# Linear attention: half heads in blocks of their own, features through device memory

## Chip, core and metric

The kernel is one program on one core of a Trainium2 chip. The metric is the device time of one execution in microseconds. PE is TensorE, DVE VectorE, ACT ScalarE, POOL GpSimd, SP SyncE, which here only issues DMAs. The granted clock is the share of TensorE's full clock.

## What is computed

Four chunks of 512 tokens go through a block of a Macaron shape. The lines below leave out reshapes and the other layers.

```python
x = L0_attn_hidden_states                       # 4 x 512 tokens x 512
x = x + 0.5 * _L0_ffn_ref(_layernorm(x), ...)   # spline lookup
x = x + _L0_attn_ref(_layernorm(x), ...)        # linear attention: what the change touches
x = x + 0.5 * _L0_ffn_ref(_layernorm(x), ...)
x = x + 0.5 * _L1_ffn_ref(_layernorm(x), ...)   # Hadamard feed-forward
x = x + _L1_attn_ref(_layernorm(x), ...)        # differential softmax attention
x = x + 0.5 * _L1_ffn_ref(_layernorm(x), ...)

def _L0_attn_ref(hidden_states, Wq, bq, Wk, bk, Wv, bv, Wo, bo, rand_matrix):
    # 16 query heads, 8 key and value heads, 32 dimensions each
    q = (hidden_states @ Wq.T + bq) ...; k = ... ; v = ...
    q = q * cos + _rotate_half(q) * sin         # halves of 16: concat(-x2, x1)
    k = k * cos + _rotate_half(k) * sin
    n = jnp.sqrt(jnp.sum(x * x, axis=-1, keepdims=True))
    x = x / jnp.maximum(n, 1e-06)
    p = jnp.einsum('...d,ed->...e', x, R)       # R: rand_matrix, 16 x 32
    feats = jnp.concatenate([jnp.sin(p), jnp.cos(p)], axis=-1) / math.sqrt(F)
    kv = jnp.einsum('bhsf,bhsd->bsfd', kp, v)   # per token, over the heads
    out = jnp.einsum('bhsf,bsfd->bhsd', qp, kv)
    return out @ Wo.T + bo
```

## The kernel before

The program keeps all 2048 tokens in SBUF and runs in three stretches. Setup (0 to 230 us) turns and mixes the weights and routes the first spline layer. The body of the linear attention runs as `b_tensor`, `b_vector`, `b_scalar`, `b_pool`, `b_sync`, called with i = -1 to 3 (b_sync with 0 to 3). The rest, from about 750 us, is the second layer (`solo_*`, `c_*`), 67% of the span.

Every engine's instruction order is written out by hand and semaphores join them. A run i has up to four roles (`b_roles`): the chunk `now` = i is scored and written out, `new` = i + 1 is projected and turned into features, `look` = i + 2 goes through the first spline layer, and `back` = i - 1 is routed for the next one.

A run has two parts. The y-loop goes over y = 0 to 16 (16 pairs of groups of 16 tokens). For `now`, at each y TensorE makes scores (L1299), VectorE masks them (L1623, same token only), and at y + 1 TensorE weights the values (L1312) into one PSUM bank, `SUM_BANK`; every four y ScalarE and VectorE read it as high and low halves (`sums`, L1455 and L1631), for which `weighted` waits. For `new`, TensorE computes six projections of 128 rows, first the keys' two blocks, then the queries' four (`project`, 12 f16 matmuls in L1184). ScalarE adds the bias (L1461), TensorE swaps the half heads with a constant matrix (`rotate`, L1330), GpSimd multiplies by the cosines (L1549), VectorE by the sines and adds (`rope`, L1638 and L1639), GpSimd squares (L1552), and TensorE sums the squares per head (`length`, L1336). Then `lengths`, `inverse` (Ln, Exp on ScalarE) and `refine` (L1643 to L1651) give the inverse lengths. VectorE's list holds, besides, the spline lookup for `look` (place at y = 6, slope at 8, value at 11) and the token sums and routing for `back` (picks at y = 1 and 2, ends at y = 3 where i >= 2).

In the tail, for each block z, TensorE spreads the inverse lengths over the rows (L1345) and projects the block on the random matrix (L1348). ScalarE copies the spread (L1475). VectorE multiplies the two and reduces the angle (`angle`, L1659, L1663, L1664), ScalarE takes the sine and the high half (L1477, L1480), VectorE the low half (`low`, L1671). Sine and cosine rows are made of one block at once, with a phase that differs by row: 16 rows of sine and 16 of cosine of each head. Between them stand the values (`value`, L1690), output rows (`output`, `residual`, L1679), the norm and the transposes of the next chunk's input (`look`; L2068, L1851) and routing for `back`. The next run's first score comes behind these on TensorE.

The features are laid from the blocks into the stacks `ks` and `qs` (three parts of 32 rows: high, high or low, low or high; heads along the free axis) by direct DMAs from SBUF to SBUF (`b_spread`, L1570): per chunk 18 on SP's queue and 18 on GpSimd's, 64 KB each. ScalarE regroups `ks` into `ksg` (`keys`, L1488). The values go out to device memory (L1605) and come back in another order (L1609) on SP's queue, between the spreads of the first and of the second half of the queries.

## Time and profile before

| | us |
|---|---|
| median of 3 runs (2273.76 to 2275.56) | 2275.51 |
| the profiled execution | 2269.64 |
| its span, first to last instruction | 2267.8 |
| TensorE busy | 1996.4 (88%) |
| VectorE busy | 1269.0 (56%) |
| ScalarE busy | 727.9 (32%) |
| GpSimd busy | 258.9 (11%) |
| granted clock, mean | 0.926 |

In timeline rows the columns are start, duration, engine, line, operation, operands, count, and in brackets the idle time before it and what ended it. An f32 matmul shows as two records. Run i = -1 has its first projection at 230 us and its first spread at 275; the first scores of i = 0, 1, 2, 3 start at 319.6, 419.5, 530.3 and 631.5 us.

### The profile page before, as it was taken

The page shows a single profiled execution, that of the slowest core. Times are in us where ns is not written, and L with a number is a line of the kernel's source. Part 1 is how long each engine was busy: PE and PEld are TensorE (multiplying, and loading weights), DVE is VectorE, ACT ScalarE, POOL GpSimd, SP SyncE. Part 2 cuts the span into 40 slices and gives each one's busy share as a digit, 9 for nine tenths or more (in the row PEclk, how much of TensorE's full clock was granted, in tenths as well). Part 3 has the DMA queues.
Part 4 walks back from the last instruction along what each step waited for, and adds up shares of the span by engine and source line. Part 5 has one row for each costly group of instructions (what it writes and reads, how often), then busy time and mean ns, then how long its engine had stood idle before and what let it go on. Part 6 is the DMA issues. An engine that isn't in the chain of part 4 may idle for free.

```text
span 2267.8 us, 29080 instructions
## 1 busy us (share of the span) xinstructions
PE 1996.4 (88%) x11854; PEld 940.2 (41%) x11854; DVE 1269.0 (56%) x2323; ACT 727.9 (32%) x1131; POOL 258.9 (11%) x236
## 2 busy tenths in 40 slices
PE   4774868887863899999999999999999999999999
PEld 3442333334332444444444444444444444444444
DVE  5777457676576455554565356636564456623322
ACT  4552242432421222232244223522343234411211
POOL 3630221322210000001000100001000100000000
PEclk7886778978966999999999999999999999999999
DMA  7224030212222222212111111111111111133321
GB/s 262 93 75 174 1 61 15 47 35 26 44 65 103 72 96 93 96 53 75 47 57 47 56 47 44 60 65 38 38 66 38 65 47 57 57 102 102 112 96 71
DMA packets 87680, 158.71 MB, mean 70 GB/s; under 512 B 44342, under 2 KB 51324, under 8 KB 82812
## 3 DMA queue, kind: packets, MB, share of 16 engines
q1 hardware_dynamic: 85244, 152.14, 21.0%
q0 software_dynamic: 2304, 4.72, 1.0%
q8 instruction: 94, 1.54, 0.3%
q14 instruction: 38, 0.31, 0.0%
HBM read 128.52 MB, written 18.87 MB: 65 GB/s over the span
## 4 chain that ended last, share of the span: by engine, by line
PE 49%; DVE 4%; ACT 2%; issue 1%; ACTq 0%; DVEq 0%
PE ps L1184 26%; PE ps L1936 12%; PE ps L2450 2%; PE ps L2469 1%; DVE arena L2614 1%; PE ps L2446 1%; PE ps L2452 1%; PE ps L2396 1%; PE ps L2487 1%; PE ps L2471 1%; PE ps L2473 1%; PE ps L2478 1%; PE ps L2476 1%; PE ps L2393 1%; DVE arena L1991 0%
## 5 line engine op out<-in xcount | busy, mean ns | idle before, releaser
L1184 PE MATMUL ps<-arena 128*128 128x512 f16 (+1 forms) x4512 | 1013.7, 379 | 22.8 <-DVE arena L1991 12.9
L1184 PEld LDWEIGHTS ps<-arena 128*128 128x128 f16 x4512 | 434.8, 98 | 541.2 <-issue 45.3
L1936 PE MATMUL ps<-arena 128*128 128x512 f16 x1536 | 343.8, 379 | 12.5 <-DVE arena L2019 9.3
L1936 PEld LDWEIGHTS ps<-arena 128*128 128x128 f16 x1536 | 146.6, 97 | 185.9 <-DVE arena L2019 12.1
L1991 DVE SCALAR_TENSOR_TENSOR arena<-arena,ps 128x512 f32<-128x512 f32 x128 | 87.9, 687 | 208.7 <-ACT arena L1958 208.1
L1958 ACT ACTIVATE arena<-ps,arena 128x512 f32<-128x512 f32 x128 | 87.8, 686 | 358.5 <-PE ps L1184 358.4
L2543 ACT ACTIVATE arena<-ps 128x1024 f32<-128x1024 f32 (+3 forms) x128 | 90.3, 706 | 254.1 <-PE ps L2452 254.1
L2648 DVE CAST arena<-arena 128x1024 f16<-128x1024 f32 (+3 forms) x128 | 66.2, 517 | 150.4 <-ACT arena L2543 148.3
L2614 DVE TENSOR_REDUCE arena<-ps 128x2 f32<-128x256 f32 (+3 forms) x128 | 99.6, 820 | 65.0 <-PE ps L2396 65.0
L2019 DVE SCALAR_TENSOR_TENSOR arena<-ps,arena 128x512 f32<-128x512 f32 x64 | 44.0, 688 | 134.5 <-PE ps L1936 134.3
L2000 DVE SCALAR_TENSOR_TENSOR arena<-ps,arena 128x512 f32<-128x512 f32 x128 | 95.8, 748 | 39.1 <-PE ps L1184 39.0
L2650 DVE TENSOR_TENSOR arena<-arena 128x1024 f16<-128x1024 f32 (+3 forms) x128 | 111.4, 871 | 4.4
L2594 POOL TENSOR_TENSOR arena<-arena 128x512 f16<-128x512 f32 x32 | 37.1, 1160 | 624.9 <-ACT arena L2521 624.9
L1982 DVE TENSOR_TENSOR arena<-arena 128x512 f16<-128x512 f32 x128 | 90.9, 711 | 4.0 <-ACT arena L1950 4.0
L1950 ACT ACTIVATE arena<-arena 128x512 f16<-128x512 f32 x128 | 79.8, 624 | 17.5 <-DVE arena L2000 17.5
L2598 POOL TENSOR_TENSOR arena<-arena 128x512 f32<-128x512 f32 x16 | 19.0, 1187 | 581.5 <-DVE arena L2661 581.5
L1851 PE MATMUL ps<-arena 128*128 128x128 f32 x192 | 33.2, 333 | 55.1 <-ACT arena L2068 55.1
L1623 DVE TENSOR_TENSOR arena<-ps,arena 128x256 f32<-128x256 f32 x128 | 47.9, 417 | 56.4 <-PE ps L1299 55.7
L2450 PE MATMUL ps<-arena 32*128 32x512 f16 (+3 forms) x768 | 72.9, 293 | 0.0
L2518 ACT ACTIVATE arena<-ps 128x512 f32<-128x512 f32 x32 | 19.1, 598 | 166.6 <-PE ps L1184 166.6
L731 PE MATMUL ps<-arena 128*128 128x128 f32 x240 | 44.1, 325 | 31.6 <-DVE arena L968 18.9
L1312 PE MATMUL ps<-arena 128*32 128x64 f32 x1024 | 41.9, 294 | 28.3 <-DVE arena L1623 14.3
(268 smaller groups left out, 2435.4 us busy)
## 6 DMA issues: line engine op xcount, KB each, us to landing
arena<-wug_dram SPq DMA_DIRECT2D x128, 512.0 KB, 3.3
arena<-wd_hi_dram SPq DMA_DIRECT2D x16, 1024.0 KB, 5.0
arena<-wd_lo_dram SPq DMA_DIRECT2D x16, 1024.0 KB, 7.3
wug_dram<-arena SPq DMA_DIRECT2D x4, 2048.0 KB, 15.7
arena<-arena SPq DMA_DIRECT2D x72, 64.0 KB, 2.9
arena<-arena POOLq DMA_DIRECT2D x72, 64.0 KB, 2.7
arena<-_attn_hidden_states_dram SPq DMA_DIRECT2D x4, 1024.0 KB, 12.3
arena<-in_L_ffn_W_up_dram SPq DMA_DIRECT2D x8, 512.0 KB, 5.0
```

The source lines that it names most:

```text
L1184: ins = pe.matmul(out, left[a](c), right[b](c), start=(at == 0), stop=(at == 3 * n - 1))
L1936: ins = pe.matmul(k.ps[:, bank, :], act[x][:, slot, cols], wd[y][:, f, :], start=(f == 0 and m == 0), stop=(f == 7 and m == 2))
L1950: e.activation(k.act_hi[:, g % ACT_SLOTS, :], k.prod[:, g % 2, :], ACT.Copy).then_inc(s["f_hi"], 1)
L1958: e.activation(k.th[:, g % 2, :], k.ps[:, GATE_BANK, :], ACT.Tanh, scale=k.wscale[:, FB + a:FB + a + 1])\
L1982: e.tensor_tensor(k.act_lo[:, g % ACT_SLOTS, :], k.prod[:, g % 2, :], k.act_hi[:, g % ACT_SLOTS, :], ALU.subtract)\
L1991: e.scalar_tensor_tensor(out=th, in0=th, scalar=1.0, in1=k.ps[:, GATE_BANK, :], op0=ALU.add, op1=ALU.mult)\
L2000: e.scalar_tensor_tensor(out=k.prod[:, g % 2, :], in0=k.ps[:, UP_HALF_BANK, :], scalar=k.wscale[:, a:a + 1], in1=th, op0=ALU.mult, op1=ALU ...
L2450: pe.matmul(k.ps[:, bank, queries], x[rows, 4 + b, keys], y[rows, b, queries], start=False, stop=False)
L2543: e.activation(k.p32[:, t % 2, :, queries], k.ps[:, 0:2, queries], ACT.Exp, scale=SCORE).then_inc(s["c_exp"], 1)
L2614: e.tensor_reduce(k.mx[:, u, 4 * b + 2 * j:4 * b + 2 * j + 2], k.ps[:, bank:bank + 2, 0:(u + 1) * P], AXX, ALU.max).then_inc(s["c_max"], 1)
L2648: e.tensor_copy(k.p_hi[:, t % 2, :, queries], k.p32[:, t % 2, :, queries]).then_inc(s["c_p_hi"], 1)
L2650: e.tensor_tensor(k.p_lo[:, t % 2, :, queries], k.p32[:, t % 2, :, queries], k.p_hi[:, t % 2, :, queries], ALU.subtract).then_inc(s["c_p_l ...
```

## The change

Each projection block now holds one half (16 dimensions) of eight heads: `halves_of` reorders the rows of the query and key weights and of their biases at load. A pair of blocks (a = 0 keys, 1 and 2 queries) holds the two halves of the same heads on the same partitions. So the rotation needs no matmul: VectorE reads the projection in PSUM twice, adding the bias and multiplying by cosine and sine (with the scale folded into the tables), and GpSimd adds or subtracts across the pair. The projection on the random matrix is two matmuls that accumulate, for eight heads; the groups a = 0 and 1 are issued at y = 14 and 15. One product with the lengths serves sine block and cosine block, which are blocks of their own with a phase each. The lengths are spread for three pairs instead of six blocks.

Features go to the stacks through a tensor `feat` in device memory: a store per block and part, a load per stack part, the load waiting for its stores. SP carries the high parts, GpSimd the low parts. On SP the values are stored behind the third and fourth block's stores and loaded behind the sixth's, before the last queries' loads. ScalarE's keys(2) and keys(3) stand behind the last feature. The sums use two banks in turn.

```diff
-    parts = [("ident", ident), ("had", had), ("rot", rot), ("cos", np.cos(ang)),
+    parts = [("ident", ident), ("had", had), ("cos", np.cos(ang) * unit),
...
-    load_nat(0, [(rows_of(d["L0_attn_Wq"])[:, 0:2], 2), (rows_of(d["L0_attn_Wq"])[:, 2:4], 2)])
-    load_nat(1, [(rows_of(d["L0_attn_Wk"]), 2), (rows_of(d["L0_attn_Wv"]), 2)])
+    load_nat(0, [(halves_of(d["L0_attn_Wq"], z), 1) for z in range(4)])
+    load_nat(1, [(halves_of(d["L0_attn_Wk"], z), 1) for z in range(2)] + [(rows_of(d["L0_attn_Wv"]), 2)])
...
-    for j in range(8):
-        sp.dma_start(k.rt[32 * (j // 2):32 * (j // 2) + 32, 16 * j:16 * j + 16],
-                     d["L0_attn_rand_matrix"].rearrange("e d -> d e")).then_inc(s["b_in"], 16)
+    for h in range(8):
+        for half in range(2):
+            sp.dma_start(k.rt[16 * h:16 * h + 16, half, 16 * h:16 * h + 16],
+                         d["L0_attn_rand_matrix"].rearrange("e d -> d e")[16 * half:16 * half + 16])\
+                .then_inc(s["b_in"], 16)
...
+    V.link(e.tensor_scalar(k.bqk, k.bqk, W_SCALE * A_SCALE, None, ALU.mult))
...
-SUM_BANK = 5
+SUM_BANK = (4, 5)
-ROT_BANK = 4
-LAST_BANK, LAST_KEY = (2, 3), 4
+LAST_BANK, LAST_KEY = (2, 3), 7
-ROT_AT = (2, 3, 5, 6, 8, 9)
+TURN_AT = (14, 15)
...
-        if y % 4 == 0 and y:
-            pe.wait_ge(s["b_ot_lo"], TPC * now + y // 4)
+        if y % 4 == 0 and y >= 8:
+            pe.wait_ge(s["b_ot_lo"], TPC * now + y // 4 - 1)
...
         if t >= 2:
-            pe.wait_ge(s["b_qf"], 6 * new + t - 1)
+            pe.wait_ge(s["b_rope"], 6 * new + t - 1)
...
-    def rotate(z):
-        pe.wait_ge(s["b_qf"], 6 * new + z + 1)
-        need(pe, s["b_rope"], 6 * new + z)
-        pe.matmul(k.ps[:, ROT_BANK, :], k.c["rot"], k.qf[:, z, :], start=True, stop=True).then_inc(s["b_rot"], 1)
...
-    def turns(z):
-        if new is None:
-            return
-        if z == 0:
+    def turned(a):
+        pe.wait_ge(s["b_rot"], 6 * new + 2 * a + 2)
+        if a == 0:
+            pe.wait_ge(s["b_rope"], 6 * (new + 1))
+        else:
+            need(pe, s["b_y"], 3 * new + a - 1)
+        for half in range(2):
+            ins = pe.matmul(k.ps[:, PROJ_BANK[a % 2], :], k.rt[:, half, :], k.qr[:, 2 * a + half, :], start=(half == 0),
+                            stop=(half == 1))
+        ins.then_inc(s["b_proj"], 1)
+
+    def spread(a):
+        if a == 0:
             pe.wait_ge(s["b_r"], new + 1)
-        need(pe, s["b_spread"], 6 * new + z)
-        pe.matmul(k.ps[:, WIDE_BANK, :], k.spread[:, z * P:(z + 1) * P], k.r2, start=True, stop=True).then_inc(s["b_p"], 1)
-        if z >= 2:
-            pe.wait_ge(s["b_y"], 6 * new + z - 1)
-        pe.matmul(k.ps[:, PROJ_BANK[z % 2], :], k.rt, k.qr[:, z, :], start=True, stop=True).then_inc(s["b_proj"], 1)
+            if now is not None:
+                pe.wait_ge(s["b_ot_lo"], TPC * now + 3)
+        need(pe, s["b_spread"], 3 * new + a)
+        pe.matmul(k.ps[:, WIDE_BANK, :], k.spread[:, a * P:(a + 1) * P], k.r2, start=True, stop=True).then_inc(s["b_p"], 1)
...
-    for z in range(4):
-        turns(z)
-        value(z)
-    turns(4)
+    if new is not None:
+        spread(0)
+    value(0)
+    value(1)
+    if new is not None:
+        spread(1)
+    value(2)
+    value(3)
+    if new is not None:
+        spread(2)
+        turned(2)
     output(0)
-    turns(5)
     output(1)
...
 # b_scalar, tail
-    for z in range(4):
-        turns(z)
+    spread(0)
+    feature(0)
+    spread(1)
+    feature(1)
+    feature(2)
+    spread(2)
+    feature(3)
+    feature(4)
     keys(0)
     keys(1)
-    turns(4)
+    feature(5)
     keys(2)
     keys(3)
-    turns(5)
...
 # b_pool
+        for a in range(3):
+            e.wait_ge(s["b_rope"], 6 * new + 2 * a + 2)
+            for half, op in enumerate((ALU.subtract, ALU.add)):
+                z = 2 * a + half
+                e.tensor_tensor(k.qr[:, z, :], k.qr[:, z, :], k.qf[:, 2 * a + 1 - half, :], op).then_inc(s["b_rot"], 1)
+            for z in (2 * a, 2 * a + 1):
+                e.wait_ge(s["b_rot"], 6 * new + z + 1)
+                need(e, s["b_nsum"], 6 * new + z - 1)
+                e.tensor_tensor(k.q2[:, z % 2, :], k.qr[:, z, :], k.qr[:, z, :], ALU.mult).then_inc(s["b_sq"], 1)
+        b_low_spread(k, e, new)
...
+def b_store(k, eng, part, z, sem):
+    f = (k.f_hi, k.f_lo)[part]
+    eng.dma_start(k.d["feat"][part, z // 2][:, z % 2], f[:, z, :]).then_inc(sem, 16)
+
+def b_load(k, eng, part, a, rows, sem):
+    stack, heads = (k.ks, slice(0, 8)) if a == 0 else (k.qs, slice(8 * a - 8, 8 * a))
+    eng.dma_start(stack[32 * rows:32 * rows + 32, heads, :], k.d["feat"][part, a].rearrange("h s e t -> (s e) h t"))\
+        .then_inc(sem, 16)
+
+def b_low_spread(k, e, i):
+    need(e, s["b_qs2"], 32 * i)
+    for a in range(3):
+        for z in (2 * a, 2 * a + 1):
+            e.wait_ge(s["b_f_lo"], 6 * i + z + 1)
+            b_store(k, e, 1, z, s["b_lo_out"])
...
+        e.wait_ge(s["b_lo_out"], 96 * i + 32 * (a + 1))
+        b_load(k, e, 1, a, 1 if a else 2, s["b_qs2" if a else "b_ks2"])
...
 # b_sync
+    for a in range(3):
+        for z in (2 * a, 2 * a + 1):
+            sp.wait_ge(s["b_f_hi"], 6 * i + z + 1)
+            b_store(k, sp, 0, z, s["b_hi_out"])
...
+        if a == 1:
+            need(sp, s["b_s"], PAIRS * i)
+            sp.wait_ge(s["b_v_in"], TPC * (i + 1))
+            need(sp, s["b_vr"], 128 * i)
+            sp.dma_start(scratch.rearrange("(u p) n -> p u n", p=P), k.v0).then_inc(s["b_v_out"], 16)
+        if a == 2:
+            need(sp, s["b_pv"], PAIRS * i)
+            sp.wait_ge(s["b_v_out"], 16 * (i + 1))
+            for h in range(8):
+                sp.dma_start(k.vr[GROUP * h:GROUP * h + GROUP], scratch[:, 32 * h:32 * h + 32]
+                             .rearrange("(g t) d -> t g d", t=GROUP)).then_inc(s["b_vr"], 16)
+        sp.wait_ge(s["b_hi_out"], 96 * i + 32 * (a + 1))
+        for rows in ((0, 2) if a else (0, 1)):
+            b_load(k, sp, 0, a, rows, s["b_qs" if a else "b_ks"])
...
 # b_vector
     def rope(z):
-        e.wait_ge(s["b_rot"], 6 * new + z + 1)
-        e.wait_ge(s["b_cos"], 6 * new + z + 1)
-        V.link(e.tensor_tensor(k.qf[:, z, :], k.ps[:, ROT_BANK, :], k.c["sin"], ALU.mult))
-        e.tensor_tensor(k.qr[:, z, :], k.qr[:, z, :], k.qf[:, z, :], ALU.add).then_inc(s["b_rope"], 1)
+        e.wait_ge(s["b_qk_done"], 6 * new + z + 1)
+        if z == 0:
+            need(e, s["b_proj"], 3 * new)
+        bias = k.bqk[:, ORDER[z]:ORDER[z] + 1]
+        for to, table in ((k.qr, "cos"), (k.qf, "sin")):
+            ins = e.scalar_tensor_tensor(out=to[:, z, :], in0=k.ps[:, PROJ_BANK[z % 2], :], scalar=bias, in1=k.c[table],
+                                         op0=ALU.add, op1=ALU.mult)
+        ins.then_inc(s["b_rope"], 1)
...
     def angle(z):
...
+        a, half = z // 2, z % 2
+        ang, turns = k.ang[:, half, :], k.turns[:, a % 2, :]
+        if half == 0:
+            e.wait_ge(s["b_proj"], 3 * new + a + 1)
+            e.wait_ge(s["b_spread"], 3 * new + a + 1)
+            e.scalar_tensor_tensor(out=turns, in0=k.ps[:, PROJ_BANK[a % 2], :], scalar=float(1 / (2 * np.pi)), in1=turns,
+                                   op0=ALU.mult, op1=ALU.mult).then_inc(s["b_y"], 1)
+            e.wait_ge(s["b_y"], 3 * new + a + 1)
         need(e, s["b_f_lo"], 6 * new + z - 1)
-        V.link(e.tensor_scalar(ang, turns, k.c["phase"], ROUND, ALU.add, ALU.add))
+        V.link(e.tensor_scalar(ang, turns, PHASE[half], ROUND, ALU.add, ALU.add))
...
-            if y - 1 in ROT_AT:
-                rope(ROT_AT.index(y - 1))
+            if y - 1 in QK_AT:
+                rope(QK_AT.index(y - 1))
...
+        d["feat"] = nc.dram_tensor("feat_dram", (2, 3, 8, 2, 16, CH), F16).ap()
```

## Rows read from the trace of the kernel before

**Rows 1.** Windows: stretch, length, busy us of each engine (instructions), clock, DMA share, GB/s.
```profile
core 0: us, PE busy (x) PEld busy (x) DVE busy (x) ACT busy (x) POOL busy (x), PEclk, DMA share, GB/s
319.60:376.00 56.40, 47.76 (x409) 21.45 (x412) 33.17 (x75) 8.28 (x13) 13.04 (x12) 0.91 0.00 1
530.30:588.00 57.70, 47.39 (x369) 18.65 (x368) 38.23 (x84) 10.62 (x19) 12.58 (x12) 0.87 0.00 1
631.50:672.00 40.50, 24.46 (x333) 14.77 (x336) 31.40 (x80) 9.04 (x16) 0.00 (x0) 0.58 0.01 1
750.00:2267.00 1517.00, 1469.19 (x8698) 665.82 (x8696) 780.12 (x1299) 464.91 (x722) 75.76 (x64) 1.00 0.20 67
```

**Rows 2.** Timeline of SP's queue in the setup.
```profile
7.41 0.92 SPq L627 DMA_DIRECT2D arena<-in_L_attn_Wq_dram  x2
163.55 7.09 SPq L667 DMA_DIRECT2D arena<-_L_attn_rand_matrix_dram  x8
198.00 0.52 SPq L651 DMA_DIRECT2D wd_hi_dram<-arena  x1
```

**Rows 3.** Timeline of the y-loop of i = 0, PE and POOL.
```profile
328.20 1.13 PE L1330 MATMUL ps<-arena 128*128 128x512 f32 x2
330.05 2.77 PE L1184 MATMUL ps<-arena 128*128 128x512 f16 x12
331.75 1.04 POOL L1552 TENSOR_TENSOR arena<-arena 128x512 f32<-128x512 f32 x1 [5.88 <-DVE arena L1639]
332.74 1.09 POOL L1549 TENSOR_TENSOR arena<-arena 128x512 f32<-128x512 f32 x1
...
357.82 0.67 PE L1312 MATMUL ps<-arena 128*32 128x64 f32 x16 [2.08 <-DVE arena L1631]
359.90 2.05 PE L1330 MATMUL ps<-arena 128*128 128x512 f32 x2 [1.41 <-DVE arena L1639]
370.96 0.64 PE L1312 MATMUL ps<-arena 128*32 128x64 f32 x16 [2.34 <-DVE arena L1631]
376.25 1.12 PE L1345 MATMUL ps<-arena 24*128 24x512 f32 x2
```

**Rows 4.** Timeline: first spreads, a rotation, an angle, a first score of other runs.
```profile
274.95 2.07 PE L1345 MATMUL ps<-arena 24*128 24x512 f32 x2 [4.65 <-DVE arena L1651]
550.39 2.05 PE L1330 MATMUL ps<-arena 128*128 128x512 f32 x2 [5.96 <-DVE arena L1639]
590.09 2.07 PE L1345 MATMUL ps<-arena 24*128 24x512 f32 x2
594.21 0.69 DVE L1659 SCALAR_TENSOR_TENSOR arena<-ps,arena 128x512 f32<-128x512 f32 x1 [2.65 <-PE ps L1348]
631.48 1.03 PE L1299 MATMUL ps<-arena 96*128 96x256 f16 x4
```

**Rows 5.** Timeline of the tail of i = 0: VectorE, ScalarE and the next first score.
```profile
378.79 0.69 DVE L1659 SCALAR_TENSOR_TENSOR arena<-ps,arena 128x512 f32<-128x512 f32 x1 [1.09 <-PE ps L1348]
...
404.06 1.99 ACT L1488 ACTIVATE arena<-arena 96x1024 f16<-96x1024 f16 x2
406.63 0.69 DVE L1659 SCALAR_TENSOR_TENSOR arena<-ps,arena 128x512 f32<-128x512 f32 x1 [1.76 <-ACT arena L1475]
409.36 0.63 ACT L1480 ACTIVATE arena<-arena 128x512 f16<-128x512 f32 x1
410.03 0.69 DVE L1671 SCALAR_TENSOR_TENSOR arena<-arena 128x512 f16<-128x512 f32 x1 [0.85 <-ACT arena L1480]
419.50 0.38 PE L1299 MATMUL ps<-arena 96*128 96x256 f16 x2 [0.21 <-issue]
```

**Rows 6.** DMA issues: tensors, queue, count, KB each, median us from issue to landing.
```profile
arena<-arena SPq DMA_DIRECT2D x72, 64.0 KB, 2.9
arena<-arena POOLq DMA_DIRECT2D x72, 64.0 KB, 2.7
values_dram<-arena SPq DMA_DIRECT2D x4, 512.0 KB, 3.1
arena<-values_dram SPq DMA_DIRECT2D x32, 64.0 KB, 4.1
```

**Rows 7.** Timeline of SP's queue, the loads of the values in i = 0.
```profile
407.85 4.01 SPq L1609 DMA_DIRECT2D arena<-values_dram  x8
```

More of the change, by code:

```diff
@@ L41 @@
 BIG = 1.0e30
+PHASE = (0.0, 0.25)
 def host_constants():
@@ L1647, in refine @@
         e.wait_ge(s["b_n"], new + 1)
-        need(e, s["b_p"], 6 * new)
+        need(e, s["b_p"], 3 * new)
         V.link(e.tensor_tensor(t, n2, r0, ALU.mult))
```

170 lines of the change are left out of this document (66 added, 104 removed).

## Prediction

> **What bounds the kernel now.** I read the stage windows first. From 750 us to the end TensorE is busy 1469.2 of 1517 us at a full clock, and no line of that part changes [rows 1]. What the change touches lies between 230 and 672 us: the five runs of the linear-attention body, i = -1 to 3. Each is a y-loop (scores, masks, sums of one chunk beside projections of the next) and a tail (features, spreads, output rows, next transposes). In the y-loop of i = 0 TensorE is busy 47.8 of 56.4 us, VectorE 33.2; in that of i = 3, which has no new chunk, VectorE 31.4 of 40.5 [rows 1]. So with a new chunk the order on TensorE sets the loop, with VectorE not far behind. In the tails TensorE has room and VectorE's in-order stream does not: from the first angle to its last low half it runs 378.79 to 410.72, and what interrupts it is ScalarE [rows 5]. The chain of waits on the page reaches back only to about 985 us, so for this stretch I use the timeline.
>
> **Change part by part.**
>
> *Rotation.* Six `rotate` matmuls (L1330) per new chunk go. A pair of f32 records takes 1.13 us at full clock and 2.05 at half [rows 3], so i = 0 loses about 5 x 1.1 + 2.05 = 7.6 us of TensorE time and the 1.41 us wait in front of the last one. The six ScalarE evacuations (L1461) go as well. VectorE keeps twelve passes a chunk: two fused reads of PSUM per block replace two passes. The new form is that of L1659, 0.69 us [rows 5], like the pass it replaces. GpSimd keeps twelve passes at 1.04 to 1.09 us [rows 3], but four now follow each pair of blocks, 4.3 us behind the second block.
>
> *Sum banks.* Bank 5 alternates with bank 4, so `weighted` at y = 4, 8, 12 no longer waits for the sums before it. Those waits are 2.08 and 2.34 us in i = 0 [rows 3].
>
> *Projection onto the random features.* Six f32 matmuls stay, as two-matmul groups, and two of the three groups move into the loop at y = 14 and 15: four matmuls, 4 x 1.12 (form of L1345 [rows 3]) = 4.5 us on TensorE. They wait only for GpSimd's rotated halves, and lie beside the length, Ln/Exp and refine work of VectorE and ScalarE. Three of the six spread matmuls go from the tail.
>
> *y-loop of i = 0, queued by hand in the new order.* Gross 7.6 + 1.4 + 4.4 - 4.5 = 8.9 us. VectorE takes part of it back, because its lookahead work (place, slope, value) is untouched and now meets masks and rope: by my queueing the last rope pair ends at 351.6, `length(5)` at 359.9, the refinement at 366.4, `turned(1)` at 369.3, and the first spread starts at 370.0 where it was 376.25 [rows 3]. Gain 6.2 (bounds 3 and 9). i = 1 has the same order plus token sums: 6.0. i = -1 has no masks, its first spread stood at 274.95 behind the refinement [rows 4]; rope without a matmul between brings it to 267.7: 7.2. i = 2 had the longest stall: rotate(1) waited 5.96 us for VectorE, which stood in route picks and ends [rows 4]. Now rope runs in front of those ends, so projections and lengths go on: first spread at about 578.5 against 590.09, gain 11.6 (bounds 5 and 14; this is the least certain term). i = 3: no new chunk, only the bank change. VectorE is its bound, and the mask of the same y comes just ahead of the sums: 2.0 (bounds 0.5 and 4).
>
> *Tails.* The first angle needs one spread and one copy instead of spread, copy and projection: 378.79 - 376.25 = 2.5 becomes 1.8, gain 0.7 (1.3 in i = -1). Each odd block saves the product with the lengths, 0.69 plus a step: 3 x 0.7 = 2.1 us of VectorE per chunk. The 1.76 us in which angle(5) waited for ScalarE's copy goes too [rows 5]. Against this, keys(2) and keys(3), 1.99 us for two, now stand behind the last Sin and copy and in front of the table load and root that start the next transposes. From first angle to first score it was 419.50 - 378.79 = 40.7; requeued 39.3, so 1.4 each for i = -1, 0, 1. i = 2 has no scatter or norm work on VectorE, and runs at the angle-Sin-copy-low rhythm; there all of the cut shows: the start, 594.21 - 590.09 = 4.1, becomes 2.6, and 4.3 comes off the rest up to 631.48 [rows 4], gain 5.8 (bounds 2 and 8).
>
> *Features through device memory.* Instead of 36 direct spreads of 64 KB per chunk there are 12 stores of 128 KB and 9 loads of 256 KB, on the same two queues: SP issues 6 + 6 instead of 18, GpSimd 6 + 3 instead of 18. A load now waits for its store. Nearest rows: a store to the values takes 3.1 us, a load from them 4.1, a direct spread 2.9 (SP) and 2.7 (GpSimd) [rows 6]. So low half to landed stack: 0.6 + 3.1 + 0.5 + 4.1 = 8.3 us. For the keys the cover is 10 us and more: keys(0) stands behind block 4's copy. For the last queries it is thin. Name T the end of the last feature copy, 409.99 before [rows 5]. On SP the eight value loads, 4.01 us of issue [rows 7], now stand behind the last store and ahead of the query loads, which are so issued at T+5 to T+6, behind their 128-byte pieces, and land at T+10 to T+13. TensorE asks for the queries at T + 9.5 + 2.0 = T+11.5. Cost 0 to 3 us in each of i = -1, 0, 2 (in 1 the route work covers it); I take 0.5 each, 1.5, because the same 768 KB landed before that first score when issued to within 4 us of it. If the cover were gone each us of landing is a us of time.
> The trace shows 3.1 and 4.1 us for the two legs; the Trainium skill (DMA: Bandwidth & Descriptors, Anatomy of one DMA) puts about 2 us of fixed cost on each DMA, most of it the receipt from the target, longest for device memory. That speaks against this change: two such legs where one was. With 2.0 us each the way would be about 6 us, under the cover all the same.
>
> *Setup.* Three more weight loads at 0.46 us (0.92 for two), one more vector and a 0.2 us scaling: 0 to 1.9 us, I take 0.8, as the loads behind are a backlog of transfers. The eight random-matrix loads become sixteen: 7.09 us become at most 14, from 163.55, with the next issue not before 198.00 [rows 2]: hidden.
>
> **Sum.** i = -1: 7.2 + 1.3 + 1.4 = 9.9. i = 0: 6.2 + 0.7 + 1.4 = 8.3. i = 1: 6.0 + 0.7 + 1.4 = 8.1. i = 2: 11.6 + 5.8 = 17.4. i = 3: 2.0. Together 45.7, less 1.5 and 0.8: 43.4 us. The profiled execution took 2269.6 us (span 2267.8), so it would be 2226. The median of the runs shown is 2275.5, 5.9 above it; the forecast is for such a median: 2275.5 - 43.4 = 2232.
>
> **Rivals.**
> 1. *VectorE becomes the bound of the loops.* For: 38.2 of 57.7 us busy in i = 2 [rows 1], and its programme order is a fixed list in which one blocked step holds masks and rope. Against: its passes don't grow. It would hold the loops to a third of the gain (31.0 to 10), tails as forecast: 43.4 - 21 = 22, 2253.
> 2. *The last queries come late.* Landing at T+14 to T+15 costs about 3 more in three tails: 2241.
> 3. *TensorE's clock gives it back.* It was granted 0.91 in i = 0's loop and 0.58 in i = 3's, where it idled [rows 1]; a rotate at the lower of its two levels (1.2 GHz against 2.4) took 2.05 for 1.13, and a projection would take twice its 2.77 [rows 3]. If four of the six projections in each of three loops fell there: 12 x 2.8 = 34, 2266. For: a loop with fewer matmuls leaves more gaps. Against: the gaps that go are TensorE's own waits.
> 4. *Slower than before: loads move at the pace of the old pieces.* Were a 256 KB load four times a direct spread, 4 x 2.9 = 11.6 us [rows 6], and two of them served one after the other, the queries would land at T + 6 + 23 = T+29, 17.7 past the need, in four tails: 71 - 43 = 28 slower, 2303. It decides when the landing is later than T+22 (11 us a chunk). Against: bytes are not what those 2.9 us are made of, since the store of the values moves 512 KB in 3.1 us [rows 6].
> 5. *The gross gain shows in full*, as loops are less tied to VectorE than I queue them: 8.9 for 6.2 in i = 0 and so on, about 15 more: 2217.
> 6. *It does not do what it says*: scores wait anyhow for something unchanged (the transposes of the next chunk). Then only loops gain and tails nothing: 31 + 2 - 2.3, close to 2243; it lies inside the forecast.
>
> **How the numbers follow.** Forecast with 6 and its near surroundings 0.55, rival 1 0.2, rival 2 0.08, rival 3 0.05, rival 4 0.04, rival 5 0.08. Two in ten may be left out: I cut rivals 3 and 4 and the outer halves of 1 and 5. Range 2212 to 2256, which also holds the unknown costs: loops 3 to 9 and 5 to 14, landing 0 to 3 three times, setup 0 to 1.9. About 0.2%, 4.6 us, is what a measurement of this kernel can tell from no change. Faster 0.93 (all but rival 4 and a part of 3), same 0.03, slower 0.04.
>
> **What would show it.** Right: no matmul of the rotation's form; first score of i = 0 about 9 us earlier and that of i = 3 about 41 earlier; first score idle behind transposes or route work, not behind a DMA; first spread right behind the refinement or the second projection group; sums' waits gone at y = 4, 8, 12. Wrong: TensorE idle before a first score until a load of features lands; ScalarE's keys waiting on loads; VectorE without idle time through a y-loop; a granted clock below 0.85 in the loops of i = 0 to 2. The largest error would be in i = 2's loop.

## The result and the profile after

The changed kernel takes 2237.16 us (median of 4 runs, 2231.76 to 2240.6) against 2274.81 for the kernel before (4 runs): ratio 0.9834, 95% interval 0.9821 to 0.9846, a gain of 37.7 us (35 to 41). The forecast was 2232 and a gain of 43.4. The profiled execution of after took 2238.54 us (span 2236.7), that of before 2269.64, so the two profiles differ by 31.1 only; where the other 6.6 probably lie is told with the clock below.

The windows of the body and of the part that the change doesn't touch, after (columns as in [rows 1]):
```profile
core 0: us, PE busy (x) PEld busy (x) DVE busy (x) ACT busy (x) POOL busy (x), PEclk, DMA share, GB/s
237.10:274.70 37.60, 33.66 (x120) 14.10 (x120) 19.66 (x38) 1.85 (x3) 13.85 (x12) 0.86 0.00 0
315.50:367.20 51.70, 47.48 (x409) 21.86 (x409) 33.09 (x74) 3.53 (x7) 13.88 (x12) 0.90 0.01 1
509.00:561.00 52.00, 44.76 (x381) 18.24 (x380) 39.35 (x87) 6.70 (x13) 13.50 (x12) 0.89 0.01 1
596.60:637.80 41.20, 25.04 (x337) 15.25 (x338) 31.80 (x81) 9.74 (x17) 0.00 (x0) 0.58 0.02 3
720.00:2236.00 1516.00, 1468.20 (x8679) 664.96 (x8677) 778.37 (x1297) 463.52 (x721) 75.76 (x64) 0.99 0.20 67
```
The y-loop of i = 0 is 51.6 us long where it was 56.6, that of i = 2 52.1 where it was 59.8. VectorE is busy for about as long as in [rows 1] (33.1 for 33.2 us, 39.4 for 38.2), TensorE in i = 0 too (47.5 for 47.8), in a shorter loop. TensorE's waits for the low half of the sums are gone, but in i = 2 a weighted sum now waits for its mask:
```profile
526.28 0.65 PE L1322 MATMUL ps<-arena 128*32 128x64 f32 x16 [3.71 <-DVE arena L1651]
```

The timeline of after, the points that answer to [rows 4] and [rows 5] (start, duration, engine and line; L1195 is the projections' line, L1361 the spread, L1309 the score, L1498 the feature copy):
```profile
237.10 1.01 PE L1195 MATMUL ps<-arena 128*128 128x512 f16 x2 [1.50 <-DVE arena L1900]
274.75 1.12 PE L1361 MATMUL ps<-arena 24*128 24x512 f32 x2 [0.43 <-DVE arena L1683]
315.55 0.58 PE L1309 MATMUL ps<-arena 96*128 96x256 f16 x2 [0.68 <-issue]
367.16 1.12 PE L1361 MATMUL ps<-arena 24*128 24x512 f32 x2
409.60 0.38 PE L1309 MATMUL ps<-arena 96*128 96x256 f16 x2 [2.32 <-DMA arena<-feat_dram]
...
596.58 0.80 PE L1309 MATMUL ps<-arena 96*128 96x256 f16 x3 [2.47 <-DMA arena<-feat_dram]
```
From such points of both traces comes this table. T is the end of the last feature copy, as in the prediction; "feed" is TensorE's first projection behind the loop of i = 3. Gains in us, predicted and measured:

| part | before | after | predicted | measured |
|---|---|---|---|---|
| setup, to the first projection | 230.4 | 237.1 | -0.8 | -6.7 |
| loop to the first spread, i = -1 | 44.6 | 37.65 | 7.2 | 6.9 |
| the same, i = 0 | 56.6 | 51.6 | 6.2 | 5.0 |
| the same, i = 1 | 58.5 | 51.6 | 6.0 | 6.9 |
| the same, i = 2 | 59.8 | 52.1 | 11.6 | 7.7 |
| first score to feed, i = 3 | 42.5 | 41.2 | 2.0 | 1.3 |
| first spread to first angle, four times | 14.9 | 7.4 | 4.2 | 7.5 |
| first angle to T, four times | 121.2 | 101.6 | | 19.6 |
| T to the first score, four times | 45.6 | 57.5 | | -11.9 |
| the two above together (landing included) | 166.8 | 159.1 | 7.0 | 7.7 |
| sum to the feed | 674.0 | 637.8 | 43.4 | 36.2 |
| feed to the end | 1593.9 | 1599.0 | 0 | -5.1 |

From the first projection to the feed, the stretch that the change works in, 443.6 us became 400.7: 42.9 gained for 44.2 forecast. The parts are further off than their sum.

The DMA issues of after, which answer to [rows 6]:
```profile
arena<-feat_dram SPq DMA_DIRECT2D x24, 256.0 KB, 4.7
...
feat_dram<-arena POOLq DMA_DIRECT2D x24, 128.0 KB, 3.7
arena<-feat_dram POOLq DMA_DIRECT2D x12, 256.0 KB, 4.1
...
values_dram<-arena SPq DMA_DIRECT2D x4, 512.0 KB, 4.0
arena<-values_dram SPq DMA_DIRECT2D x32, 64.0 KB, 4.1
```
A store and a load of the features take 3.7 and 4.1 to 4.7 us, near the 3.1 and 4.1 taken from the values: larger DMAs are not slower in proportion to their size, and rival 4 is out.

### The profile page after: what moved, and what is told of

It is laid out like the page before. It is cut to its first block, busy times and chain, and to the rows that moved or that the text cites. A ratio compares the mean times of both kernels' runs of the same rounds, so it can differ in the third digit from the quotient of the medians.

```text
span 2236.7 us, 28766 instructions
## 1 busy us (share of the span) xinstructions
PE 1958.3 (88%) x11782; PEld 931.0 (42%) x11782; DVE 1260.7 (56%) x2312; ACT 705.0 (32%) x1095; POOL 246.1 (11%) x200
## 4 chain that ended last, share of the span: by engine, by line
PE 49%; DVE 4%; ACT 2%; issue 1%; ACTq 0%; DVEq 0%
PE ps L1195 27%; PE ps L1970 12%; PE ps L2484 2%; PE ps L2503 1%; DVE arena L2648 1%; PE ps L2480 1%; PE ps L2486 1%; PE ps L2430 1%; PE ps L2521 1%; PE ps L2505 1%; PE ps L2507 1%; PE ps L2512 1%; PE ps L2510 1%; PE ps L2427 1%; DVE arena L2025 0%
## 5 line engine op out<-in xcount | busy, mean ns | idle before, releaser
L1195 PE MATMUL ps<-arena 128*128 128x512 f16 (+1 forms) x4512 | 1017.5, 381 | 41.0 <-DVE arena L1724 18.8
L1195 PEld LDWEIGHTS ps<-arena 128*128 128x128 f16 x4512 | 434.0, 99 | 557.0 <-issue 38.5
L1970 PEld LDWEIGHTS ps<-arena 128*128 128x128 f16 x1536 | 146.6, 97 | 185.8 <-DVE arena L2053 12.1
L741 PE MATMUL ps<-arena 128*128 128x128 f32 x240 | 46.7, 340 | 35.3 <-DVE arena L979 16.4
L1651 DVE TENSOR_TENSOR arena<-ps,arena 128x256 f32<-128x256 f32 x128 | 47.2, 416 | 42.3 <-PE ps L1309 41.5
L1322 PE MATMUL ps<-arena 128*32 128x64 f32 x1024 | 41.9, 293 | 25.8 <-DVE arena L1651 25.6
```

Source lines behind the costliest of these rows:

```text
L1195: ins = pe.matmul(out, left[a](c), right[b](c), start=(at == 0), stop=(at == 3 * n - 1))
L1970: ins = pe.matmul(k.ps[:, bank, :], act[x][:, slot, cols], wd[y][:, f, :], start=(f == 0 and m == 0), stop=(f == 7 and m == 2))
```

## The experiments

Times are medians, ratios are to the kernel before as run beside each. All of them start from the changed kernel unless it is said. What each kernel's one profiled execution shows is set beside the median here, cut at the first projection and at the feed, since the stretch behind the feed takes one of two lengths some 5 us apart, whatever the edit (see the clock below); it is one execution each:

| kernel | median | first projection | from it to the feed | feed to the end |
|---|---|---|---|---|
| before | 2274.81 | 230.4 | 443.6 | 1593.9 |
| after | 2237.16 | 237.1 | 400.7 | 1599.0 |
| e_contig (1) | 2227.19 | 230.1 | 398.3 | 1593.8 |
| e_vr (2) | 2242.94 | 237.1 | 402.8 | 1598.5 |
| e_klate (2) | 2240.11 | 238.3 | 402.3 | 1598.1 |
| e_vrk (2) | 2237.63 | 236.3 | 406.6 | 1592.7 |
| e_vlast (2) | 2233.96 | 237.3 | 402.5 | 1593.8 |
| e_vlk (2) | 2230.8 | 238.6 | 396.4 | 1592.6 |
| e_reread (2) | 2229.67 | 237.7 | 392.4 | 1598.0 |
| e_onebank (3) | 2235.74 | 238.7 | 402.0 | 1593.7 |
| e_rot (4) | 2252.76 | 240.5 | 418.5 | 1598.8 |
| e_tail (5) | 2241.06 | 236.9 | 410.3 | 1592.5 |
| e_best (6) | 2225.74 | 230.4 | 398.4 | 1598.6 |
| e_warm (6) | 2222.98 | 232.5 | 396.7 | 1593.7 |

**1. The setup's loads.** In after, weights Wq and Wk come in six loads whose rows are reordered into half heads. The edit loads them as before the change and lets the evacuations of the first transposes reorder:
```diff
-    load_nat(0, [(halves_of(d["L0_attn_Wq"], z), 1) for z in range(4)])
-    load_nat(1, [(halves_of(d["L0_attn_Wk"], z), 1) for z in range(2)] + [(rows_of(d["L0_attn_Wv"]), 2)])
+    load_nat(0, [(rows_of(d["L0_attn_Wq"])[:, 0:2], 2), (rows_of(d["L0_attn_Wq"])[:, 2:4], 2)])
+    load_nat(1, [(rows_of(d["L0_attn_Wk"]), 2), (rows_of(d["L0_attn_Wv"]), 2)])
...
+    both = w0[:, :, n // 2 * 2 * P:n // 2 * 2 * P + 2 * P].rearrange("p c (s m) -> p c s m", s=2)
+    at = 64 * (n % 2)
+    return [(both[:, :, s, at:at + 64].rearrange("p c (h e) -> p c h e", e=16), s) for s in range(2)]
...
+            for to, half in first_columns(k.w0_hi, 4 * g + r):
+                ins = e.activation(to, first_source(k.ps[:, r, :], half), ACT.Copy, scale=W_SCALE)
```


> The changed kernel, but Wq and Wk are loaded as before the change (three loads of contiguous 128-row blocks instead of six reordered ones), and the reordering of the rows into half heads is done by the evacuations of the first transposes (two instructions of half the width in place of one, six times on ScalarE and on VectorE). Theory A: the 6.7 us by which the first projection comes later in the changed kernel (237.1 against 230.4) are the reordered loads, which move 195 GB/s between 10 and 15 us where the old ones moved 374. Then the first projection is back at 230.4 to 232.5 and the time is about 5 us under the changed kernel's 2237, 2232. Theory B: the delay is the issue of more DMAs and the extra vectors on SyncE's queue; three fewer loads then give back 0.5 to 1.5 us, the first projection stays above 235.


Measured: 2227.19 us, ratio 0.9794 (0.9774 to 0.9815), first projection at 230.10. The windows from 10 to 15 us of before, after and this kernel, in that order:
```profile
10.00:15.00 5.00, 4.03 (x19) 4.02 (x20) 2.13 (x9) 0.83 (x2) 0.00 (x0) 1.00 1.01 374
```
```profile
10.00:15.00 5.00, 1.86 (x8) 1.78 (x8) 2.10 (x10) 0.00 (x0) 0.00 (x0) 1.00 0.60 195
```
```profile
10.00:15.00 5.00, 3.56 (x17) 3.55 (x18) 2.08 (x10) 0.62 (x2) 0.00 (x0) 1.00 1.01 371
```
SyncE's queue of after, while they are issued:
```profile
7.71 2.63 SPq L630 DMA_DIRECT2D arena<-in_L_attn_Wq_dram  x4
...
12.16 9.81 SPq L652 DMA_DIRECT2D arena<-_attn_hidden_states_dram  x4
22.01 3.93 SPq L630 DMA_DIRECT2D arena<-in_L_attn_Wo_dram  x2
```
The last two numbers of a window are the busy share of the 16 DMA engines and GB/s: the reordered loads keep 0.60 of the engines busy and move half as much. Wo, behind them, is issued at 22.0 us for 16.4 before, and the setup never catches up: theory A. The time is 10.0 us under the changed kernel's, where 5 were expected: besides the 7 us of setup, the profiled loop of i = 0 is 3.0 us shorter (48.6), with a granted clock of 1.00 in its first 6 us where after has 0.70. No run shows whether that comes of the edit. In the nine other kernels here that load the reordered rows the first projection stands between 236.3 and 240.5, in the two others that don't at 230.4 and 232.5. The Trainium skill (DMA: Bandwidth & Descriptors, Why a DMA increments its semaphore by 16 and not by 1) says that a DMA uses as many engines, up to 16, as divide the slowest dimension of both of its access patterns. By that rule it is eight for a source ordered by eight heads first. The trace agrees with it in half the rate (195 for 374 GB/s), though no view here counts the engines; the prediction should have asked it.

**2. The last queries: order on SyncE's queue, and the copies of the keys.** In the tail of i = 0 of after:
```profile
395.79 1.99 ACT L1506 ACTIVATE arena<-arena 96x1024 f16<-96x1024 f16 x2
395.91 0.58 SPq L1586 DMA_DIRECT2D feat_dram<-arena  x1
396.59 4.99 SPq L1637 DMA_DIRECT2D arena<-values_dram  x8
397.80 1.28 ACT L2109 ACT_TABLE_LOAD   x1
...
401.63 0.97 SPq L1593 DMA_DIRECT2D arena<-feat_dram  x2
402.00 0.59 POOL L1593 DMA_DIRECT2D arena<-feat_dram  x1 [4.49 <-DMA feat_dram<-arena]
```
The query loads go out at T+5.7 behind the value loads, as predicted, and the first score waits 2.3 us for one of them (shown above). They took 5.4, 6.4 and 7.1 us from issue to landing. While the value loads' pieces are under way, the DMA share (last number but one) is over 1 and yet only 107 GB/s move, where 1.01 moved 371 to 374 in the setup:
```profile
400.00:403.00 3.00, 0.00 (x0) 0.00 (x0) 1.66 (x5) 2.44 (x4) 0.98 (x2) 0.67 1.60 107
```
First edit, the value loads ahead of the last store:
```diff
         for z in (2 * a, 2 * a + 1):
+            if z == 5:
...
+                for h in range(8):
...
             sp.wait_ge(s["b_f_hi"], 6 * i + z + 1)
             b_store(k, sp, 0, z, s["b_hi_out"])
```


> The changed kernel, but the eight value loads on SyncE's queue stand in front of the last store of high halves instead of behind it. Theory A (the last queries come late): in the tails of i = 0 and i = 2 TensorE waits 2.3 and 2.5 us for the load from device memory before the first score; with 5 us of issue out of the way the query loads are issued when the store has landed, near T+4.5 instead of T+5.7, and the wait falls to about 1 in both; the first score of i = 0 comes at T+12.4 to 12.8 instead of T+13.7, that of i = 2 at T+11.5 instead of T+12.7, i = -1 and 1 unchanged: 2.5 us in all, about 2235. Theory B (transposes and keys alone bound the start): no change in the distance from T to the first score, 2237.


Measured: 2242.94 us, ratio 0.9863 (0.9846 to 0.9879), slower if anything. T to first score: 14.2, 14.0, 19.0, 13.8 for i = -1 to 2, where after has 12.1, 13.7, 19.0, 12.7. Neither theory: in its tail of i = 0,
```profile
392.71 4.10 SPq L1626 DMA_DIRECT2D arena<-values_dram  x8
396.86 2.42 SPq L1586 DMA_DIRECT2D feat_dram<-arena  x1
403.77 0.80 SPq L1593 DMA_DIRECT2D arena<-feat_dram  x2
403.98 0.60 POOL L1593 DMA_DIRECT2D arena<-feat_dram  x1 [7.13 <-DMA feat_dram<-arena]
```
GpSimd waits 7.13 us for its store where it waited 4.49: the store, issued at the same point (T+1.0), is held up by the value loads' pieces. SyncE's own last store is late besides, since the value loads fill its queue until 396.81: it starts 1.65 us behind T for 0.03. So moving their issue forward only moves the harm.

Second edit, keys(1) to keys(3) behind the transposes:
```diff
     keys(0)
-    keys(1)
     feature(5)
-    keys(2)
-    keys(3)
...
         route_hot_scalar(k, e, back, route, BACK_BANK[0])
+    for g in range(1, 4):
+        keys(g)
```


> The changed kernel, but on ScalarE the copies of the keys' groups 1 to 3 stand behind the next chunk's transposes (the scores need them only from y = 4, 8 and 12) instead of in the tail. Theory A: ScalarE's stream from the fourth Sin to the norm write is without gaps in the changed kernel, so each of the three copies, 1.0 us each, is on the path to the transposes: T comes 1 us earlier and the transposes 3 us earlier, but the last queries' landing, T+12 to T+13, then ends the wait: the first scores of i = -1, 0 and 2 come about 1 us earlier (by the T that moved), that of i = 1, where route work ends it, 1 to 3 us. Together 3 to 5 us, about 2233. Theory B: VectorE's stream, not ScalarE's, carries the tail: nothing changes, 2237.

> Both edits: value loads in front of the last store, and the copies of the keys' groups 1 to 3 behind the transposes. If the two waits in front of the first score (last queries, ScalarE's chain to the transposes) hide each other, the sum of the two is more than each alone: first score 2 to 3 us earlier in i = -1, 0, 1 and 2.4 in i = 2, together 8 to 11 us, about 2228. If they are independent the gain is the sum of the two single runs.


Measured: 2240.11 us, ratio 0.9846 (0.9832 to 0.9861), and 2237.63 for both edits, 0.9841 (0.9826 to 0.9856). With late copies alone the waits for the query loads ahead of the first scores grow to 3.9, 4.0 and 3.2 us (i = -1, 0, 2), and the first score stands at T+13.4, 13.3, 17.0 and 12.9; with both edits they are 5.1, 5.2 and 4.4, at T+14.3, 14.2, 17.0 and 14.1. So the transposes are no longer what is late, the load is. Only the tail of i = 1, which waits for route work, gains 2.0 us. The loop behind it, that of i = 2, is 1.0 us longer (53.1 for 52.1); the loop of 54.5 us for 51.6 is that of i = 1 itself, ahead of this tail (the expectation of e_vlk puts it behind). Both kernels with late copies have that 54.5, and both start this loop at half clock behind 4 to 5 us of waiting for the load: the granted clock of its first 6 us is 0.50 where after has 1.00, and in e_klate its first projection takes 5.32 us for 2.77. So a longer wait before the first score seems to cost time behind it too; no run varies the wait alone.

Third edit, the value loads behind the last query loads; and that with the late copies:
```diff
         if a == 2:
...
-            for h in range(8):
-                sp.dma_start(k.vr[GROUP * h:GROUP * h + GROUP], scratch[:, 32 * h:32 * h + 32]
-                             .rearrange("(g t) d -> t g d", t=GROUP)).then_inc(s["b_vr"], 16)
         sp.wait_ge(s["b_hi_out"], 96 * i + 32 * (a + 1))
         for rows in ((0, 2) if a else (0, 1)):
             b_load(k, sp, 0, a, rows, s["b_qs" if a else "b_ks"])
+        if a == 2:
...
+            for h in range(8):
...
```


> The changed kernel, but the eight value loads stand on SyncE's queue behind the two last query loads. Theory A (what holds the first score is the transfer of the eight value loads, in pieces of 128 bytes, which shares the DMA engines with the last stores and query loads; moved in front of the store they lengthened its way to 7.1 us from 4.5): the query loads are issued when the store has landed, T+4 to T+5, beside nothing, and land by T+10; the first score of i = 0 comes at T+11.6 instead of T+13.7, bound by the transposes, that of i = 2 at T+10.5 to 11 instead of T+12.7, with no DMA in front of either, 4 to 5 us in all, about 2233; the values land at T+13 to T+14, when the first weighted sum wants them. Theory B (two legs through device memory take 12 us by themselves): the first scores stay at T+13 to T+14, and the weighted sums wait for the values in addition, 2 to 4 us in each of three tails: 2245.

> The same, and the copies of the keys' groups 1 to 3 behind the transposes. In i = 1 that alone brought the first score from T+19.0 to T+17.0, and the y-loop behind it took 54.5 us for 51.6. Theory A (one wait hid the other, the queries no longer do): first score at T+10 in i = -1 and 0, T+10.5 in i = 2, T+17 in i = 1; 3 us more than the kernel with the value loads last in i = -1 and 0 each. If the loops keep their length the time is 2225; if the loops give back what the tails gain, as they did with the copies alone (i = 1: 2.0 gained, 2.9 lost), it is within 3 us of the kernel with the value loads last.


Measured: 2233.96 us, 0.9823 (0.9806 to 0.9839), and 2230.8, 0.9817 (0.9793 to 0.9841): in the direction of theory A, but the intervals overlap with the changed kernel's, and the first is no shorter between first projection and feed (402.5 for 400.7). The tails are clearer. With the value loads last GpSimd waits 2.72 us for its store (i = 0):
```profile
400.92 0.60 POOL L1593 DMA_DIRECT2D arena<-feat_dram  x1 [2.72 <-DMA feat_dram<-arena]
```
SyncE's two query loads then take 3.2 and 4.5 us. No first score waits for a DMA, and it stands at T+11.2, 13.7, 19.0, 10.4 (i = 0 is told under hardware): theory A for what held it. But the loops of i = 0 and 1 are 1.3 and 2.8 us longer than after's, with a granted clock of 0.59 and 0.57 in their first 6 us for 0.70 and 1.00, which takes back the gain. With the late copies too: T+11.1, 11.1, 16.5, 11.4, which is 7.4 us of tails; but the first weighted sum of i = 3 now waits 3.92 us for the values:
```profile
596.23 0.67 PE L1322 MATMUL ps<-arena 128*32 128x64 f32 x16 [3.92 <-DMA arena<-values_dram]
```
And while the loop of i = 0 is 1.7 us shorter, those of i = 1 to 3 are 1.6, 0.7 and 2.5 us longer.

Last, the same kernel with the store's receipt taken out of the way of the last queries:


> The kernel with the value loads last and the late copies of the keys (2231), but the last query loads read block pair 1 of the feature tensor instead of pair 2, so they need not wait for the stores just issued; all stores are still made, and waited for at the end of each tail. The last queries are so those of other heads. Theory A (the way through device memory holds the first score by its two legs, and the store's receipt is 3.5 to 4.3 us of it): the wait for a load before the first scores of i = -1 and 2, 1.9 and 1.7 us, goes, as does nothing else: 3 to 4 us, about 2227. Theory B (not the receipt but the other transfers under way delay the landing): the loads are issued 3 us earlier, still land at the same time, and nothing changes.


Measured: 2229.67 us, 0.9802 (0.9785 to 0.9819). T+9.8 and 10.1 in i = -1 and 2, 1.3 us earlier each, with 0.3 and 1.0 us of waiting left; but T+12.4 in i = 0, with a wait of 3.3, later than with the receipt. Between the theories: SyncE's two query loads go out about 3 us earlier (T+0.65 for T+3.4 in i = 0) and have landed by T+7.4 there. What the first score then waits for is GpSimd's load, issued at T+2.8 behind the first value loads, which took 9.3 us and landed at T+12.1. So the receipt can go and bring 1.3 us at best, as loads, stores and value pieces are then under way together.

**3. The second bank for sums.**
```diff
-SUM_BANK = (4, 5)
+SUM_BANK = (5, 5)
...
-        if y % 4 == 0 and y >= 8:
-            pe.wait_ge(s["b_ot_lo"], TPC * now + y // 4 - 1)
+        if y % 4 == 0 and y:
+            pe.wait_ge(s["b_ot_lo"], TPC * now + y // 4)
```


> The changed kernel with one bank for the sums, as before the change (bank 5 alone, each fourth weighted sum waits for the low half of the sums before it). Theory A (TensorE's order sets the loops): the waits at y = 4, 8, 12 come back, 2.1 to 2.3 us for two of them in i = 0 before, so the loops of i = 0, 1 and 2 grow by 3 to 4.5 us each and that of i = 3 by 1 to 2: 2248. Theory B (the loops are tied to VectorE): TensorE waits at the sums and so less at its other waits, and each loop grows by less than 1.5: 2240.


Measured: 2235.74 us, 0.9834 (0.982 to 0.9849), the ratio of the changed kernel. Loops 37.6, 51.3, 53.0, 52.8 and 41.1. What TensorE's weighted sums (L1322) wait for over the whole body, with one bank and then in after (total, times, longest; L1651 is the mask, L1659 the low half of the sums):
```profile
PE ps L1322 <- DVE arena L1659: 15.9, 7, 3.5
PE ps L1322 <- DVE arena L1651: 12.7, 8, 4.2
```
```profile
PE ps L1322 <- DVE arena L1651: 25.6, 17, 4.2
```
28.6 us against 25.6: with the second bank TensorE waits for the mask instead, which stands on VectorE next to the sums. Theory B: against after the loops of i = 0 to 3 change by -0.3, +1.5, +0.7 and -0.1 us. The change's wait removed was worth nothing that shows in the time.

**4. The price of TensorE's time in the loop.**
```diff
+        pe.matmul(k.ps[:, PROJ_BANK[t % 2], :], k.c["had"], k.c["cos"], start=True, stop=True)
         cols = slice(ORDER[t] * P, (ORDER[t] + 1) * P)
```


> The changed kernel with six matmuls of the removed rotation's shape and type (128x128 f32 against 512 f32 columns) put back for each new chunk, ahead of each of the six projections, into the bank that the projection then overwrites. They compute nothing that is used. Theory A (TensorE's order sets the loops): each costs its 1.1 us, 6.7 us a loop in i = -1 to 2, 27 us together: 2264. Theory B (VectorE sets them as much as TensorE does): part of it falls into TensorE's waits, and the four loops grow by 2 to 4 us each: 2249.


Measured: 2252.76 us, 0.9912 (0.9892 to 0.9932). The loops grow by 2.3, 4.1, 4.9 and 4.5 us, 15.9 in all, for 24 matmuls of 1.12 us or more, 27 us. So a us of TensorE time is worth 0.6 us here: 2252.76 is nearer to theory B's 2249 than to theory A's 2264, though three loops grow by a little more than B's 2 to 4. The matmuls put back wait for nobody; the old rotation's waits for ScalarE and VectorE are not in this price.

**5. Where the random-feature projections stand.**
```diff
-TURN_AT = (14, 15)
+TURN_AT = ()
...
         spread(0)
+        turned(0)
     value(0)
     value(1)
     if new is not None:
         spread(1)
+        turned(1)
```


> The changed kernel with the projections onto the random features of blocks 0 to 3 back in the tail, behind the first and the second spread, as before the change (they stood in the loop at y = 14 and 15). Theory A (TensorE's order sets the end of the loop in full): the loops lose 4.0 to 4.5 us each in i = -1 to 2, the first angle comes 2.5 to 4.1 us behind the first spread instead of 1.85, so 0.7 to 2.3 us of it return: 6 to 14 us faster in all, near 2228. Theory B (the refinement on VectorE sets the first spread and the four matmuls lie beside it): the loops lose 1 us or less, the tails gain 0.7 to 2.3 each: 2238 to 2242.


Measured: 2241.06 us, 0.9854 (0.984 to 0.9869). The interval overlaps the changed kernel's at its edge; the profiled execution is 9.6 us longer than after's between first projection and feed. The loops get shorter by 0.0, 4.5, 0.1 and 1.8 us and the first angle comes 5.8, 5.8, 4.7 and 5.8 us behind the first spread, 4.0, 4.0, 2.9 and 4.0 later. In i = -1 of this kernel:
```profile
274.59 2.07 PE L1361 MATMUL ps<-arena 24*128 24x512 f32 x2 [4.72 <-DVE arena L1685]
276.59 3.78 PE L1351 MATMUL ps<-arena 128*128 128x512 f32 x4
```
TensorE waits 4.72 us for the refinement, the place where after has the four matmuls, and does the first two behind it at half clock (3.78 us for these two matmuls, four records, against 1.99 at the full clock in after's loop of i = 2). The first score of i = 3 comes 9.1 us later. Theory B in the loops of i = -1 and 1, A in that of i = 0, and i = 2 between them; the loss in the tail is more than either had.

**6. Together.** The edits of experiment 1, the value loads last and the late copies; and that with matmuls of no use in TensorE's idle time before the transposes:
```diff
+        for _ in range({0: 7, 1: 3}.get(new, 0)):
+            pe.matmul(k.ps[:, NEXT_TURN[0], :], k.c["had"], k.c["cos"], start=True, stop=True)
```


> The three edits together: Wq and Wk loaded in contiguous blocks and reordered by the evacuations, the value loads behind the last query loads, and the copies of the keys' groups 1 to 3 behind the transposes. Setup and body have no queue in common at those places, so the gains should add: 7 us of setup (first projection at 230 to 231) on top of the kernel with the other two edits (2231): 2221 to 2224, the first score of i = 3 near 583. If the body gives it back (its loops vary by 2 to 3 us with the clock that they start at) it is 2227.

> The kernel with those three edits, and TensorE given f32 matmuls (128x128 against 512 columns) that compute nothing used, in the tails of i = -1 (seven) and i = 0 (three), in the idle time ahead of the next chunk's transposes, 14.6 and 3.9 us there. Theory A (the idle time ahead of the transposes is what brings the granted clock to 0.60 to 0.72 in them and in the first 6 us of the loop): the transposes and the first scores and projections run at the full level and the loops of i = 0 and 1 are 2 to 3 us shorter, 4 to 6 in all. Theory B (the clock is not decided there, or the loops' length is VectorE's): no gain, and up to 2 us more where the added matmuls run at the lower level and are not done when the transposes could start.


Measured: 2225.74 us, 0.9791 (0.9777 to 0.9806), and 2222.98, 0.9778 (0.976 to 0.9796). Both lie within the interval of experiment 1: with the setup mended, the tails' edits add nothing that shows, although the first scores come at T+10.8, 10.7, 17.0 and 10.8. From first projection to feed the first takes 398.4 us, experiment 1's kernel 398.3. The loop of i = 0 is 53.5 us, where that of experiment 1 is 48.6. Its start, TensorE in the kernel with the three edits:
```profile
307.85 2.76 PE L1210 MATMUL ps<-arena 128*128 128x512 f16 x12
310.45 0.38 PE L1324 MATMUL ps<-arena 96*128 96x256 f16 x2
313.18 0.67 PE L1337 MATMUL ps<-arena 128*32 128x64 f32 x16 [2.35 <-DMA arena<-values_dram]
313.78 4.06 PE L1210 MATMUL ps<-arena 128*128 128x512 f16 x12
```
The first weighted sum waits 2.35 us for the values, and the projection behind that wait takes 4.06 us where the one before took 2.76: the clock falls too. The added matmuls raised the clock of the stretch before the first score of i = 0 (0.77 for 0.56), but the first 6 us of that loop then ran at 0.61 (0.95 without): the loops of i = 0 and 1 stayed at 52.6 and 53.3 (53.5 and 53.1 without), theory B.

## Why the prediction was right, and where it was not

The forecast was a gain of 43 with a range of 19 to 63; 37.7 was measured. Its mechanisms were there; several sizes were not. That the stretch from first projection to feed came out at 42.9 for 44.2 is in part luck: the loops fell 5.2 short, and the spread-to-angle part went 3.3 over. Of the signs named, the rotation's matmuls and the waits for the sums are gone, but the first score of i = 0 came 4.1 us earlier for 9 (setup took the rest) and that of i = 3 34.9 for 41, and one sign of being wrong did show: in i = 0 and 2 TensorE was idle before a first score until a load of features landed.

- *Setup* was the mis-sized term, 6.7 us for 0.8 (bounds 0 to 1.9). The step counted instructions on a queue and took the loads behind as a backlog that moves as fast as before. Experiment 1 shows that the form of the loads halved the rate, and undoing that alone brings the first projection back to 230.1.
- *Loops* gained 27.8 for 33.0. Removing the rotation is worth something, as told: at 0.6 per us (experiment 4), 7.6 us of matmuls are worth 4.6, and the four loops got 15.9 us longer with such matmuls put back. Against that stand the projections moved in, 4.5 us of i = 0's loop by experiment 5, so these two don't add up to the 5.0 that i = 0 gained, and no run splits the rest, the rotation's waits among it. The sum banks' part was wrong: 4.4 us of waits in i = 0 counted as gross gain, worth nothing there (experiment 3). i = 3, priced by the banks alone at 2.0, gained 1.3, and not by the banks: with one bank again it is as long (41.1). What gave it is open. The largest error was where the text put it, in i = 2, 7.7 for 11.6: the rotation's 5.96 us wait [rows 4] is gone, but a weighted sum waits 3.71 us for its mask (shown above), which stands on VectorE behind a route pick, rope and the token sums. Rival 1 is true by a part.
- *From spread to angle* 7.5 for 4.2: the first angle's gain in i = -1 to 2 was 2.3, 0.7, 2.3, 2.3. It was costed as one copy and one spread less; in three of four tails the old chain ran at half clock (two of them in [rows 4]: 2.07 us for a spread), where after's first spread takes 1.12, and experiment 5 shows two f32 matmuls in that place costing 2.9 to 4.0 us.
- *From angle to score* 7.7 for 7.0, by the predicted trade: VectorE's shorter stream brings T 4.3 us nearer to the first angle (6.7 in i = 2), and the keys behind it cost about 2 of that in i = 0 and 1.
- *The last queries* were costed at 0.5 three times. The issue at T+5.7 and the need at T+11.4 were as told; the landing was T+13.7 in i = 0, so rival 2's 2.3 and 2.5 us came true in i = 0 and 2, and nothing in i = -1. The step that was off is the landing: 4.1 us, the median of the 64 KB value loads, for 256 KB loads that share the engines with those 512 KB in pieces of 128 bytes. In i = 0 they took 5.4 to 7.1 us; with the values behind them SyncE's two took 3.2 and 4.5.
- *The clock* (rival 3) is neither in the forecast nor nothing. From the feed to the end before took 1593.9 us and after 1599.0, with the same instructions. Over all fourteen traces this part takes 1592.5 to 1593.9 (before, and experiments e_contig, e_vrk, e_vlast, e_vlk, e_onebank, e_warm, e_tail) or 1598.0 to 1599.0 (after, e_vr, e_klate, e_rot, e_best, e_reread), and nothing between. Two kernels that have that part in common, e_vlast and then e_vr:
```profile
707.97 3.65 PE L1885 MATMUL ps<-arena 128*128 128x128 f32 x16 [20.04 <-ACT arena L2102]
713.03 15.75 PE L1195 MATMUL ps<-arena 128*128 128x512 f16 x72 [1.41 <-DVE arena L1900]
```
```profile
708.48 3.65 PE L1885 MATMUL ps<-arena 128*128 128x128 f32 x16 [20.05 <-ACT arena L2102]
713.54 17.24 PE L1195 MATMUL ps<-arena 128*128 128x512 f16 x72 [1.42 <-DVE arena L1900]
```
After the same 20 us of idle time the same 72 matmuls take 1.5 us more: the granted clock stays at its lower level (1.2 GHz) until 716.6 us in e_vr and until 712.4 in e_vlast. Some 225 us later it falls again, for 6.8 us in e_vr and 3.4 in e_vlast, and near 1416 us for another 3.4 in e_vr alone. All six longer traces have this pattern and none of the eight shorter ones. The profiled execution of before fell into the shorter case and that of after into the longer, which fits the profiles differing by 31.1 and the medians by 37.7: up to the feed the gain is 36.2. The other executions left no trace, so this is not shown. What decides the case is open; e_vrk and e_vr, e_vlk and e_best, in the body near relatives, fall on either side.

## What to carry to other kernels

When a layout moves into a load, ask what dimension comes first in it on either side: here it cost half the rate of those loads, and an evacuation did the same reordering on the way for nothing that shows. A wait that goes is worth only what the next wait in line leaves; before counting it, look at what the same engine would wait for instead. And before a DMA is moved ahead to hide it, ask whose engines it will be using there.
